# Copying the rows of each quad into a small ring before the scores load them, with fourteen staging slots in place of sixteen

## What is computed

```python
bilinear = jnp.einsum('bie,ied->bid', feature, weight)   # each row times its own 64x64 matrix
out = jnp.einsum('bid,bjd->bij', bilinear, feature)      # 200x200 scores of each sample
```

## Time and profile before

| | |
|---|---|
| median of 3 runs | 1518.4 us (1517.48 to 1518.64) |
| profiled execution | 1516.77 us, of which the span of the trace is 1514.9 us |
| TensorE busy | 1452.9 us (96%), weight loads 1206.3 us (80%) |
| VectorE busy | 1167.2 us (77%) |
| ScalarE busy | 893.5 us (59%) |
| GpSimd busy | 294.3 us (19%), 512 DMA issues |
| DMA | 438.67 MB, mean 290 GB/s; TensorE clock granted in full |

### The profile page before, as it was taken

The page is one execution under the profiler, slowest core; times in us unless marked ns, Lnnn a source line. Parts: engine busy times, 40 slices in busy tenths (PEclk is TensorE's granted clock), DMA queues, the critical chain, the costliest instruction groups (busy, mean ns, idle before and its releaser), DMA issues.

```text
span 1514.9 us, 41346 instructions
## 1 busy us (share of the span) xinstructions
PE 1452.9 (96%) x16192; PEld 1206.3 (80%) x16192; DVE 1167.2 (77%) x2048; ACT 893.5 (59%) x1313; POOL 294.3 (19%) x518
## 2 busy tenths in 40 slices
PE   7999999999999999999999999999999999999965
PEld 6888887888788787888778888788787888878754
DVE  0578778788777778778787787877877777887897
ACT  5665665656656565665656656566665656656532
POOL 0112112121221212122121121221212111121222
PEclk9999999999999999999999999999999999999999
DMA  8799999999999999999999999999999999999898
GB/s 220 225 289 288 305 300 290 299 288 304 300 290 296 294 300 292 303 290 287 290 294 303 294 295 305 292 297 292 296 299 292 301 284 305 298 292 297 265 275 257
DMA packets 308574, 438.67 MB, mean 290 GB/s; under 512 B 56480, under 2 KB 255136, under 8 KB 308384
## 3 DMA queue, kind: packets, MB, share of 16 engines
q1 hardware_dynamic: 283808, 422.80, 87.1%
q0 software_dynamic: 24576, 13.24, 6.0%
HBM read 108.13 MB, written 327.68 MB: 288 GB/s over the span
## 4 chain that ended last, share of the span: by engine, by line
PE 83%; DVE 10%; DMA 3%; issue 3%; SPq 1%; ACT 0%; POOLq 0%
PE ps L225 43%; PE bp L209 24%; PE tp L193 14%; DVE staging L256 4%; DMA x<-feature_dram 3%; DVE win L305 3%; DVE win L312 2%; PE ps L209 1%; DVE win L313 1%; PE ps L193 1%; SPq L143 0%; SPq L138 0%; SPq L131 0%; ACT staging L256 0%; ACT bl L279 0%
## 5 line engine op out<-in xcount | busy, mean ns | idle before, releaser
L225 PE MATMUL ps<-win,bl 64*100 64x200 f32 x8192 | 831.7, 344 | 42.8 <-DVE win L313 39.6
L225 PEld LDWEIGHTS ps<-win,bl 64*100 64x100 f32 x8192 | 696.5, 207 | 134.3 <-issue 67.1
L256 DVE COPY staging<-ps 100x800 f32<-100x800 f32 x512 | 503.9, 984 | 252.2 <-PE ps L225 252.2
L256 ACT COPY staging<-ps 100x800 f32<-100x800 f32 x512 | 423.3, 827 | 251.9 <-PE ps L225 251.9
L176 POOL DMA_DIRECT2D out_dram<-staging x512 | 293.6, 573 | 1213.3 <-DVE staging L256 985.5
L209 PE MATMUL bp<-xt,w 64*64 64x128 f32 x6144 | 419.6, 276 | 0.0
L209 PEld LDWEIGHTS bp<-xt,w 64*64 64x64 f32 x6144 | 326.7, 133 | 65.2 <-issue 65.2
L279 ACT COPY bl<-bp 128x512 f32<-128x512 f32 x384 | 225.2, 586 | 178.0 <-PE bp L209 178.0
L269 ACT COPY xt<-tp 128x512 f32<-128x512 f32 x384 | 225.1, 586 | 171.4 <-PE tp L193 171.4
L305 DVE COPY win<-xt 128x400 f32<-128x400 f32 x512 | 272.9, 533 | 64.5 <-ACT xt L269 48.8
L193 PE MATMUL tp<-ident,x 128*128 128x128 f32 x1536 | 252.9, 287 | 7.9 <-DMA x<-feature_dram 7.6
(11 more groups left out here) (5 smaller groups left out, 0.6 us busy)
## 6 DMA issues: line engine op xcount, KB each, us to landing
out_dram<-staging SPq DMA_DIRECT2D x1024, 300.0 KB, 4.7
x<-feature_dram SPq DMA_DIRECT2D x400, 256.0 KB, 5.1
out_dram<-staging POOLq DMA_DIRECT2D x512, 25.0 KB, 4.6
w<-weight_dram SPq DMA_DIRECT2D x24, 128.0 KB, 3.9
w<-weight_dram SPq DMA_DIRECT2D x2, 64.0 KB, 3.3
```

Of the source, the lines that this page charges most:

```text
L225: last = nc.tensor.matmul(ps[s % TILES][0:FH, h, F * b:F * (b + 1)], rows_of_bl(n, R * k + PB * i + b)[64 * h:64 * h + 64], win[64 * h:64 ...
L256: copy(staging[:, slot, :, :, :].rearrange("p b h j -> p h b j"), ps[s % TILES][0:FH, :, 0:PB * F].rearrange("p h (b j) -> p h b j", j=F)) ...
```

## The change

GpSimd gets a second task. A new ring `rows` holds the bilinear rows of three quads (`RSLOTS`), each sample's 100 rows side by side whatever the layout of `bl` in that block. `fill_rows(q)` copies the rows of quad q, 128 partitions by 400 elements, from `bl` into a slot, once the scores of the quad that last used the slot are done. Two quads are filled before the loop, and in the loop `fill_rows(q + 2)` stands ahead of the store of quad q. The scores take their weights from `rows`, and the first matmul of a quad waits for `rows_filled` too; the wait for the whole of `bl` moves to GpSimd. ScalarE's copy into `bl` waits for `rows_filled` in place of `scores_done`. `staging` has 14 slots.

```diff
-    OSLOTS = 16
+    OSLOTS = 14
+    RSLOTS = 3
...
+        rows = sbuf("rows", [128, RSLOTS, R, FH])
...
-        def rows_of_bl(n, b):
-            return bl[:, 0:FH, b] if n % 2 == 0 else bl[:, b, 0:FH]
+        def quad_of_bl(n, k):
+            quad = slice(R * k, R * (k + 1))
+            return bl[:, 0:FH, quad].rearrange("p m r -> p r m") if n % 2 == 0 else bl[:, quad, 0:FH]
...
-            for s in range(1, BLOCKS * SETS_B, 2):
-                store_rest(s)
+            def fill_rows(q):
+                n, k = q // QUADS, q % QUADS
+                if k == 0:
+                    pool.wait_ge(bl_stored, (n + 1) * NG)
+                if q >= RSLOTS:
+                    pool.wait_ge(scores_done, 2 * (q - RSLOTS) + 2)
+                nc.gpsimd.tensor_copy(rows[:, q % RSLOTS, :, :], quad_of_bl(n, k)).then_inc(rows_filled, 1)
+
+            for q in range(RSLOTS - 1):
+                fill_rows(q)
+            for q in range(BLOCKS * QUADS):
+                if q + RSLOTS - 1 < BLOCKS * QUADS:
+                    fill_rows(q + RSLOTS - 1)
+                store_rest(2 * q + 1)
...
             def scores(n, k, i):
                 s = n * SETS_B + 2 * k + i
-                if k == 0 and i == 0:
-                    pe.wait_ge(bl_stored, (n + 1) * NG)
                 if i == 0:
+                    pe.wait_ge(rows_filled, n * QUADS + k + 1)
                     pe.wait_ge(win_filled, n * QUADS + k + 1)
...
-                                                rows_of_bl(n, R * k + PB * i + b)[64 * h:64 * h + 64],
+                                                rows[64 * h:64 * h + 64, (n * QUADS + k) % RSLOTS, PB * i + b, :],
...
-                    act.wait_ge(scores_done, (n - 1) * SETS_B + 2 * t + 2)
+                    act.wait_ge(rows_filled, (n - 1) * QUADS + t + 1)
```

More of the change, by code:

```diff
@@ L41, in feature_interaction @@
     assert 2 * E == 128 and B % NB == 0 and FH % C == 0 and NG <= QUADS and R == 2 * PB
-    assert PB * F <= 512 and C * NB == 512 and OSLOTS % 2 == 0 and (BLOCKS * SETS_B) % OSLOTS == 0
+    assert PB * F <= 512 and C * NB == 512 and OSLOTS % 2 == 0
     feature_v = feature.rearrange("b f e -> b (f e)")
@@ L87, in feature_interaction @@
         bl_stored = sem("bl_stored")
+        rows_filled = sem("rows_filled")
         own_filled = sem("own_filled")
```

## The result

The changed kernel takes 1595.3 us (median of 4 runs, 1594.6 to 1595.8) against 1517.9 for the kernel before in the same comparison: ratio 1.051, 95% interval 1.049 to 1.053. It is slower by 77 us. The forecast was 1503, in a range up to 1530.

The account below looks back on a forecast made before the run. TensorE was taken to set the pace in most quads, VectorE in 103. From the profiled 1516.8 us, - 19.3 + 1.1 + 3 gave 1501.6; with that execution 1.6 below the median, the forecast was 1503, range 1496 to 1530.

Parts of the forecast that it names:

- The gain: Score weight loads in the eight even blocks: contiguous weights let them run as the odd ones, 19.3 us saved.
- GpSimd's copies: 512 copies of 400 elements on GpSimd: 0.7 us each in odd blocks, 1.0 in even; they fit below 1.06.
- The first quad: Start of the first scores: a strided copy now stands after ScalarE's last copy into `bl`, +1.1 us once.
- VectorE beside the copies: Block ends, VectorE's stage: copy after L313 under the staging copy, may hold L305 by 0.1; with late stores +3 us.
- the 0.84 us of slack: Quads where TensorE sets the pace: VectorE needs 2.30 us against 3.14, so 0.84 us per quad is free.
- VectorE is held by the copies: Rival, 0.24: GpSimd copies block VectorE's `win` copies; at 1.5 us, L305 waits 0.57 us on 103 quads, 1559 us.
- the main line of the prediction: Likeliest case, 0.58: whole kernel at 1497 to 1508 us, the new copies nearly free beside VectorE.
- Fourteen slots: Staging ring: a slot comes round after seven quads, 16.1 us, against 0.97 of copy and 4.7 of landing; no cost.
- The rival on the transfers: Rival, 0.12: at the odd pace throughout, DMA queues never drain and input groups land late; half the gain lost, 1512 us.

## Why the prediction was wrong, step by step

*The gain* had the right cause, and its size came out smaller in the time. 19.3 us were forecast. With the ring filled once, undisturbed even blocks go from 93.2 to 90.5 us, 21.6 us over eight of them, but the median is only 14 us lower (by its interval, 9 to 19). In the profiled run seven of the fifteen blocks before the last took longer than 90.5, by 10 us together, and TensorE's waits for input groups below fit that. The Trainium skill's rule ("TensorE: Matmul & The Clock Gate", LDWEIGHTS) that a load's time goes with its columns alone does not hold in this case: 207 ns for the mix of strided and contiguous weights, 162 for contiguous ones, at the same 100 columns and the same clock.

*GpSimd's copies* were sized somewhat high: 0.7 and 1.0 forecast, 0.52 and 0.87 measured alone, both short of the 1.06 us that would still fit. The stride costs 0.35 us in 400 elements, 0.9 ns each. The Trainium skill ("GPSIMD Engine Reference", Performance pitfalls) has 2.9 against 1.9 cycles, and its one cycle between them, 0.83 ns if one reckons with 1.2 GHz as the prediction did (an estimate), agrees roughly. Its levels do not: from 400 to 800 contiguous elements a copy grows by 0.34 us, 0.85 ns or one such cycle each, and not 1.9, and from 200 to 400 strided ones by 0.36 us, 1.8 ns or 2.2 cycles, and not 2.9.

*The first quad*: +1.1 forecast; TensorE began its scores 1.14 us after the last copy into `bl` in place of 0.05.

*The step that failed* is "VectorE beside the copies": "if it must let L313 end, it runs from +1.4 under the staging copy". GpSimd's strided copy does not let L313 end. It starts right behind the store, and L313, whose record began 0.25 us earlier, stands until it is over, 0.94 us a quad. A term of +3 us stood there; it measured about +91 (1595.3 against the 1504.1 with the ring filled once). The term failed in place too: it was laid on L305, which follows the staging copy, and on the 40 quads at the ends of the even blocks only. At 3.24 us VectorE is above TensorE's 3.14 in nearly every quad of the even blocks: the 0.84 us of slack that the prediction counted on there is used up, and the gain disappears with it.

*The rival* "VectorE is held by the copies" had the mechanism, at 0.24. Its sentence that a copy which got in ahead of L313 would cost 0.4 to 0.7 us a quad and 40 to 70 us in all names what happened, though too small: it is 0.94 a quad in the even blocks, most of them quads where the prediction gave the pace to TensorE, and 91 in all. It was left outside the range because its main reading set the limit by length, 1.1 us, and the main line of the prediction took L313, whose record in the earlier trace rows begins ahead of the store's end, to come first. The start of a record was the wrong thing to read. A guess that would fit, and that no run shows, is that the store is in the cross copy's way until it ends: L313 takes 0.43 us where the store's last 0.3 us run beside it, and 0.37 without a store. But behind the same store the contiguous copy of 400 came second. The Trainium skill ("SBUF — State Buffer", Who interferes with whom) says that a GpSimd instruction and a VectorE copy in a two-port mode exclude each other for the whole instruction, and that whoever issues first wins; that the copy's length decides, as the prediction drew from it, it does not say, and the memset of 0.45 us shows otherwise. The runs agree where GpSimd comes first, and on the staging copy out of PSUM being free of it. They do not agree in full where VectorE does (the cross copy takes 0.6 us and not 0.43) or in the few meetings that harm neither, and they add that the record's start does not tell who was first.

*Two more terms.* Fourteen slots cost nothing, as forecast. The rival on the transfers (0.12) said that input groups would land late at the faster pace. TensorE's idle time ahead of the transposes until an input group landed, in the kernel before, in the one before with fourteen slots, in the one with the ring filled once, and in the one with the wait:

```profile
PE tp L193 <- DMA x<-feature_dram: 7.6, 4, 5.7
```
```profile
PE tp L193 <- DMA x<-feature_dram: 13.9, 16, 5.7
```
```profile
PE tp L210 <- DMA x<-feature_dram: 14.4, 16, 6.0
```
```profile
PE tp L212 <- DMA x<-feature_dram: 21.1, 25, 5.7
```

(us in total, times, longest.) Some groups land late in the faster kernels, and that fits what is missing from the gain. It is not shown that the faster pace is the cause: the second line is of a kernel at the old pace (1521.8 us in this run), and the kernel before has itself a spread of 9 us over 23 runs (1512.7 to 1522.1), as the faster ones have 7 to 12. What would lift it was not tried.

*Still open*: what decides between the two outcomes for a given kind of GpSimd instruction. A contiguous copy of 400 never came first in 480 meetings; one of 800, a strided one of 400 out of the scratch tensor and a memset did in 442 of 455, 442 of 455 and 478 of 479, at the same starts, 0.22 to 0.30 us after the cross copy's. A near tie is suggested only for the copy of 200. Whether the store right ahead of the copy plays a part was not tried, by a copy ahead of the store or a pause between them.

## What to carry to other kernels

A copy put on an idle GpSimd can stop an SBUF-to-SBUF copy of VectorE that runs beside it; look at what VectorE does in exactly that stretch. In this kernel the GpSimd work cost almost nothing once a wait had put it under VectorE's reads of PSUM. When two records overlap by 0.2 us, price both orders, and put both into the range. And a long wait for the new step, here TensorE's 83 us for `rows`, may be a consequence: the run that made the copies with no matmul waiting for them lost just as much.

## What was not expected of the hardware

A wait added to GpSimd's queue made a kernel 90 us faster. Beside the end of GpSimd's store the cross copy takes 0.43 us, without one 0.37, while the first cross copy, which runs beside the store's start, takes 0.37 either way. A memset of 0.45 us, which reads nothing, held a VectorE copy for 0.5 us. And ScalarE needed 0.90 us for the copy of 400 strided elements that GpSimd makes in 0.87, where its copies of 512 elements out of PSUM take 0.59.
